# A decoder layer's attention, cross-attention and routed feed-forward on one core: packed score and value matmuls, folded norms, routing weights on the other side of the down projection

## What is computed

```python
x = x + _L0_attn_ref(_layernorm(x, axis=-1), L0_attn_Wqkv, L0_attn_bqkv, L0_attn_Wo, L0_attn_bo)
x = x + _L0_xattn_ref(_layernorm(x, axis=-1), ctx_1024, ctx_1024, L0_xattn_wq, L0_xattn_wk, L0_xattn_wv, L0_xattn_wo)
x = x + _L0_ffn_ref(_layernorm(x, axis=-1), L0_ffn_gate_w, L0_ffn_w_up, L0_ffn_w_down, L0_ffn_expert_bias)
...
scores = jnp.einsum('bhsd,bhtd->bhst', q, k) * (1.0 / math.sqrt(hd))
attn = jax.nn.softmax(scores, axis=-1)
vals = jnp.einsum('bhst,bhtd->bhsd', attn, v)
...
corr = jnp.fft.irfft(jnp.fft.rfft(Q, axis=-1) * jnp.conj(jnp.fft.rfft(K, axis=-1)), n=Lv, axis=-1)
top_vals, top_idx = jax.lax.top_k(corr, k_top)
...
w_t = jnp.sum(jnp.where(sel == e, top_scores, 0.0), axis=-1)
xe = xf * w_t[:, None]
h = jnp.square(jax.nn.relu(xe @ wu.T))
return (acc + h @ wd.T, None)
```

## Time and profile before

| | before |
|---|---|
| device time, median of 3 runs | 168.37 us (168.25 to 173.48) |
| span of the profiled execution | 171.5 us |
| PE busy | 153.6 us (90%), 1504 instructions |
| PEld busy | 128.2 us (75%) |
| DVE busy | 117.5 us (68%), 376 instructions |
| ACT busy | 72.5 us (42%), 153 instructions |
| POOL busy | 37.8 us (22%), 68 instructions |
| first `up` matmul starts | 93.55 us |

### The profile page before, as it was taken

How to read it: one execution, slowest core, us unless ns; L and a number is a source line. 1 busy time by engine, 2 the same in 40 slices (tenths; PEclk the granted TensorE clock), 3 DMA queues, 4 the chain that set the end, 5 groups by cost and what they waited for, 6 DMA issues and landing times.

```text
span 171.5 us, 3956 instructions
## 1 busy us (share of the span) xinstructions
PE 153.6 (90%) x1504; PEld 128.2 (75%) x1504; DVE 117.5 (68%) x376; ACT 72.5 (42%) x153; POOL 37.8 (22%) x68
## 2 busy tenths in 40 slices
PE   0439999999989987889997999999999999999992
PEld 0209777987978975478985799777998788978981
DVE  1197549676199699999989857684789856736340
ACT  2001422545544133544274960545506447347250
POOL 7126111020952201601420240005024120200000
PEclk9999999955799999999999999999999999999999
DMA  5996000000000000000000000000000010011001
GB/s 120 315 381 248 4 0 0 4 0 2 4 0 4 0 4 2 0 6 0 4 0 0 4 2 4 0 2 0 4 0 0 0 31 6 2 31 34 0 0 31
DMA packets 4391, 5.34 MB, mean 31 GB/s; under 512 B 380, under 2 KB 3708, under 8 KB 4116
## 3 DMA queue, kind: packets, MB, share of 16 engines
q1 hardware_dynamic: 3796, 3.95, 6.8%
q10 hardware_dynamic: 576, 1.14, 2.3%
HBM read 4.56 MB, written 0.52 MB: 30 GB/s over the span
## 4 chain that ended last, share of the span: by engine, by line
PE 70%; DVE 19%; issue 4%; POOL 3%; ACT 2%; DMA 2%; DVEq 0%; POOLq 0%
PE ps L877 13%; PE ps L866 12%; PE ps L740 10%; PE ps L768 8%; PE ps L748 3%; PE ps L709 3%; PE ps L851 3%; DVE xn L480 2%; PE ps L756 2%; DVE negm L535 2%; DMA x_sb<-x 2%; PE ps L806 2%; PE ps L703 1%; DVE rel L659 1%; PE ps L729 1%
## 5 line engine op out<-in xcount | busy, mean ns | idle before, releaser
L877 PE MATMUL ps<-hid,wdn_sb 128*128 128x256 f32 x128 | 32.0, 385 | 0.0
L659 DVE SCALAR_TENSOR_TENSOR rel<-ps,wb_sb 128x512 f32<-128x512 f32 x32 | 21.9, 689 | 10.3 <-PE ps L866 4.5
L740 PEld LDWEIGHTS ps<-feat 8*64 8x64 f32 x512 | 20.4, 165 | 7.1 <-DVE feat L521 4.2
L740 PE MATMUL ps<-feat 8*64 8x64 f32 x512 | 22.7, 255 | 3.0 <-DVE feat L521 3.0
L877 PEld LDWEIGHTS ps<-hid,wdn_sb 128*128 128x128 f32 x128 | 22.6, 190 | 3.6 <-issue 0.6
L452 ACT ACTIVATE hid<-rel 128x512 f32<-128x512 f32 x32 | 19.8, 630 | 10.1 <-PE ps L877 6.6
L866 PE MATMUL ps<-xhi,whi 128*128 128x256 f32 x64 | 20.9, 327 | 0.2 <-DVE praw L537 0.2
L866 PE MATMUL ps<-xlo,whi 128*128 128x256 f32 x64 | 17.9, 279 | 0.0
L866 PE MATMUL ps<-xhi,wlo 128*128 128x256 f32 x64 | 17.8, 279 | 0.0
L389 ACT ACTIVATE praw<-praw 128x512 f32<-128x512 f32 x16 | 10.1, 634 | 17.4 <-DVE praw L537 17.3
L535 DVE TENSOR_REDUCE negm<-ps 128x8 f32<-128x512 f32 x16 | 11.0, 686 | 9.5 <-PE ps L740 9.5
(11 more groups left out here) (112 smaller groups left out, 252.1 us busy)
## 6 DMA issues: line engine op xcount, KB each, us to landing
wup_sb<-w_up SPq DMA_DIRECT2D x1, 1024.0 KB, 11.3
wdn_sb<-w_down SPq DMA_DIRECT2D x1, 1024.0 KB, 10.1
c_sb<-ctxt SPq DMA_DIRECT2D x1, 512.0 KB, 8.7
out<-x_sb SPq DMA_DIRECT2D x4, 128.0 KB, 1.8
con<-consts ACTq DMA_DIRECT2D x1, 464.0 KB, 6.2
x_sb<-x SPq DMA_DIRECT2D x1, 384.0 KB, 9.5
wmid_sb<-w_mid ACTq DMA_DIRECT2D x1, 324.0 KB, 7.2
row_sb<-rows ACTq DMA_DIRECT2D x1, 260.0 KB, 4.9
```

The source lines that it names most:

```text
L659: nc.vector.scalar_tensor_tensor(rel[:, a % 2, :].rearrange("p (c t) -> p c t", c=2), psum(name, a).rearrange("p (c t) -> p c t", c=2), 0. ...
L740: last = mm(s_ps[cols, S * h:S * (h + 1)], feat[q:q + HD, 0, a % 2, g, h, :], feat[q:q + HD, 1, a % 2, g, h, :], start=True, stop=True)
L877: last = mm(acc_ps[:, 0:2 * P], wdn_sb[:, e, half, :], hid[:, a % 3, 2 * P * half:2 * P * (half + 1)], start=(e == 0 and half == 0), stop= ...
```

## The change

The program is written anew with one order table for each engine, and every step in them has its PSUM banks written behind it (`PE_ORDER` and its four companions). The order is no longer the same on all engines. What is computed where:

- Scores: the four strips of a chunk are one step. Its 64 matmuls go round the strips, innermost r, and the results of each strip go to a bank of its own (four banks).
- Values: the 32 `pv` matmuls go round the four groups of 32 output partitions; before, eight of one group stood in a row. The values of both column halves of a head ride in the free columns of the key's 32x32 blocks (`nat`), so that `fv` and half of `vtr` are gone, and ACT writes them into a `vkey` that POOL has zeroed once (L378).
- Softmax: for 12 of the 16 strips ACT copies the scores out of PSUM (`sev`, L363) and POOL subtracts the maximum (`psub`, L302); for the other four DVE does it as before (`ssub`). The exponential moves behind the transposes: ACT takes it straight from PSUM (L368), in place of an exponential and a copy.
- Norms: the first norm's centring is folded into the weights (`wc`: PE multiplies the weights by I - 1/128 once) and its scale into DVE's bias instruction (L488); the second's centring likewise into `wq`, its scale on ACT (`xs`, L399); the third is one ACT instruction with scale and shift for each tile (`xs3`, L422). DVE no longer normalises.
- Second block: the correlation runs as two halves of 64 rows into two banks (L759); the mixing matrix is built transposed by POOL (L309) from a DVE transpose (L585), so that `g` is gone.
- Third block: ACT does relu (L442) and square (L448); `up` weights are split by ACT and POOL alone. The down product takes the hidden units as its stationary side, four matmuls of 128 columns for each unit (L810), so that its rows are rows of x. DVE multiplies them by the squared routing weight and adds them to x (`mac`, L622, two for each unit). `wt`, `wb`, the accumulator's copy and `fin` are gone.

```diff
-                    if part == 0:
-                        pe.wait_ge(qkt_ready, 4 * (a + 1))
-                    s_ps, q = bank(name, a, part), 32 * part
+                    pe.wait_ge(done["ft"], NTH[("ft", a, 1)])
+                    bank(name, a)
                     for h in range(GROUPS):
                         for g in range(2):
-                            cols = slice(S * g, S * (g + 1))
-                            last = mm(s_ps[cols, S * h:S * (h + 1)], feat[q:q + HD, 0, a % 2, g, h, :],
-                                      feat[q:q + HD, 1, a % 2, g, h, :], start=True, stop=True)
-                    last.then_inc(score_full, 1)
+                            for r in range(QUAD):
+                                rows_r = slice(32 * r, 32 * r + HD)
+                                last = mm(psum(name, a, 0, r)[S * g:S * (g + 1), S * h:S * (h + 1)], feat[rows_r, a % 2, g, 0, h, :],
+                                          feat[rows_r, a % 2, g, 1, h, :], start=True, stop=True)
+                    last.then_inc(full[name], 1)
...
-                    for r in range(QUAD):
-                        pe.wait_ge(flip_free, QUAD * a + r + 1)
-                        for t in range(2):
-                            for i in range(PAIRS):
+                    for t in range(2):
+                        for i in range(PAIRS):
+                            for r in range(QUAD):
                                 last = mm(o_ps[32 * r:32 * r + 32, S * (PAIRS * t + i):S * (PAIRS * t + i + 1)],
-                                          vkey[:, a % 2, t, i, 32 * r:32 * r + 32], prob[:, a % 2, r, i, S * t:S * (t + 1)],
-                                          start=True, stop=True)
-                    last.then_inc(work_full, 1)
+                                          vkey[:, a % 2, t, i, r, :], prob[:, a % 2, r, i, S * t:S * (t + 1)], start=True, stop=True)
+                    last.then_inc(full[name], 1)
...
+                if name == "psub":
+                    pool.wait_ge(done["smax"], NTH[("smax", a, part)])
+                    pool.wait_ge(done["sev"], NTH[("sev", a, part)])
+                    both = praw[:, part].rearrange("p (h s) -> p h s", s=S)
+                    nc.gpsimd.tensor_tensor(both, both, negm[:, a, part, :].unsqueeze(2).broadcast_to([P, GROUPS, S]),
+                                            ALU.add).then_inc(done["psub"], 1)
...
+                if name == "wc":
+                    at = slice(A_QKV, A_Q) if a == 0 else slice(A_Q, A_GATE)
...
+                    mm(bank(name, a)[:, 0:at.stop - at.start], con[:, C_CEN:C_CEN + P], wa_sb[:, at], start=True,
+                       stop=True).then_inc(full[name], 1)
...
+                if name == "rel":
+                    u = EXPERTS * a + part
+                    act.wait_ge(full["up"], u + 1)
+                    if u >= 3:
+                        act.wait_ge(done["sq"], u - 2)
+                    nc.scalar.activation(rel[:, u % 3, :], psum("up", a, part), ACT.Relu).then_inc(done["rel"], 1)
...
-                    for half in range(2):
-                        last = mm(acc_ps[:, 0:2 * P], wdn_sb[:, e, half, :], hid[:, a % 3, 2 * P * half:2 * P * (half + 1)],
-                                  start=(e == 0 and half == 0), stop=(e == EXPERTS - 1 and half == 1))
-                    last.then_inc(down_done, 1)
...
+                    y_ps = bank(name, a, e)
+                    for t in range(2):
+                        for half in range(2):
+                            last = mm(y_ps[:, D * t:D * (t + 1)], hid[:, u % 3, 2 * P * half + P * t:2 * P * half + P * (t + 1)],
+                                      wdn_sb[:, e, half, :], start=(half == 0), stop=(half == 1))
+                    last.then_inc(full[name], 1)
...
+                        nc.vector.scalar_tensor_tensor(
+                            x12[:, 2 * a + t, :], psum("down", a, e)[:, D * t:D * (t + 1)], w2[:, a, t, e:e + 1],
+                            x12[:, 2 * a + t, :], ALU.mult, ALU.add).then_inc(done["mac"], 1)
```

```diff
+xt.0.0@0 wc.0.0@1 qkv.0.0@2 qkv.0.1@3 wc.1.0@4 xt.1.0@5 cdft.0.0@6 xt.2.0@7 qkv.1.0@0 cproj.0.0@1 qkv.1.1@2 score.0.0@4,5,3,6
...
+w8.0.0 st2.1.0 smax.3.0 smax.3.1 smax.3.2 pvt.2.0 smax.3.3 val.2.0 x2.0.0 ssub.3.0 st3.0.0 prod.1.0 x1.2.0 st2.2.0 top.1.0
```

More of the change, by code:

```diff
@@ L100 @@
[L100 to L125, removed]
@@ new lines, with steps @@
+rel.3.7 sq.3.6 sq.3.7
+"""
+POOL_ORDER = """
+zero.0.0 rs1.0.0 rs1.1.0 xb.0.0 rs1.2.0 wlo.0.0 psub.0.1 psub.0.2 psub.0.3 wlo.0.1 rs1.3.0 wlo.0.2 wlo.0.3 psub.1.1 psub.1.2
+psub.1.3 rs2.0.0 psub.2.1 psub.2.2 psub.2.3 mix.0.0 rs2.1.0 psub.3.1 psub.3.2 psub.3.3 rs3.0.0 rs2.2.0 xlo.0.0 mix.1.0 gs.0.0
+rs3.1.0 xlo.1.0 gs.1.0 mix.2.0 rs2.3.0 rs3.2.0 xlo.2.0 gs.2.0 mix.3.0 rs3.3.0 xlo.3.0 gs.3.0
+"""
+SP_ORDER = """
+sto.0.0 sto.1.0 sto.2.0 sto.3.0
+"""
+def steps(text):
+    found = []
+    for word in text.split():
+        step, _, banks = word.partition("@")
+        name, a, part = step.split(".")
+        found.append((name, int(a), int(part), tuple(int(b) for b in banks.split(",") if b)))
+    return found
@@ L142, in decoder_layer, with emptied_by @@
+def emptied_by(name, a, part, place):
+    if name == "score":
+        return ("sev" if (a, place) in BY_POOL else "ssub", a, place)
+    return (EMPTIES[name], a, part)
+def decoder_layer(nc, x, ctxt, w_cen, w_mid, w_up, w_down, rows, consts, out):
     with ExitStack() as ctx:
@@ L260, in decoder_layer @@
[L260 to L273 removed]
+        ld_x = [sem(f"ld_x{a}") for a in range(CHUNKS)]
@@ L459, in _ @@
+                if name == "sq":
+                    u = EXPERTS * a + part
+                    act.wait_ge(done["rel"], u + 1)
+                    if u >= 3:
+                        act.wait_ge(full["down"], u - 2)
+                    nc.scalar.activation(hid[:, u % 3, :], rel[:, u % 3, :], ACT.Square).then_inc(done["sq"], 1)
         @block.vector
         def _(dve):
-            chain = [0]
+            links = [0]
             def link(ins):
-                chain[0] += 1
+                links[0] += 1
@@ L808, in _ @@
-                    last.then_inc(work_full, 1)
-                if name == "g":
+                        for g in range(2):
+                            half = slice(64 * g, 64 * g + 64)
+                            last = mm(psum(name, a, 0, g)[:, 0:2 * L], prod[half, a % 2, i, :],
+                                      con[half, C_INV + 2 * L * i:C_INV + 2 * L * (i + 1)], start=(i == 0), stop=(i == 2))
+                    last.then_inc(full[name], 1)
+                if name == "ov":
+                    pe.wait_ge(done["cpe"], NTH[("cpe", a, 0)])
```

1011 lines of the change are left out of this document (476 added, 535 removed).

## The result

| | before | after |
|---|---|---|
| device time, median of 4 runs on one chip | 169.96 us (168.25 to 173.48) | 134.33 us (133.92 to 135.57) |
| ratio, 95% interval | | 0.799 (0.790 to 0.809) |
| span of the profiled execution (its own time) | 171.5 us (173.48) | 131.8 us (133.92) |
| first `up` starts | 93.55 us | 66.62 us |
| PE / DVE / ACT / POOL busy | 153.6 / 117.5 / 72.5 / 37.8 us | 114.3 / 89.7 / 77.2 / 46.9 us |

In kernel.py of the changed kernel the blank lines at the head are gone, so its lines are counted anew: scores are L692, values L718, `corr` L759, `up` L799, `down` L810 (PE), the accumulation with routing weights L622 (DVE), relu L442 and square L448 (ACT), the subtractions L302 (POOL).

What follows compares the result with a forecast made beforehand. The prediction took TensorE to bound the kernel, in work and clock speed: first stage 67, second stage 62 and end 2.6 make 131.6, forecast 131 us. The range for 8 in 10 was 121 to 149.

Steps and rivals of the forecast that it cites:

- 67 + 62 + 2.6: Whole kernel: first stage until the first up, second stage until the last down, then the end; 131.6 us together.
- I sum against 171.5 and give the forecast as the median: Whole kernel: terms summed against the profiled span, said to be 3.1 us above the runs' median of 168.37.
- foretold as 107 us: TensorE's work in the whole kernel at full clock: falls from 138 to 107 us, by 31.
- issue bound of 0.028 us: Scores and values: TensorE takes no instruction faster than 0.028 us; 8 us more, result 140; chance 0.20.
- The rule of the Trainium skill that was weighed: Scores: start-to-start never below about 25 ns, so 3.2 us a chunk instead of 2.0, sum about 137.
- 48 us of work at full clock, 12.7 lost at half clock, 6 idle: First stage: TensorE starts at 6 us, runs at half clock until 31.5, and ends its work at 67.
- From 6 us on as now: First stage: TensorE's 48 us of work would begin at 6 us, as in the kernel before.
- what would show it wrong: TensorE's clock: durations of equal instructions showing half clock after 35 us would be one sign against the forecast.
- later than DVE's 62, so PE's 67 counts: First stage: VectorE's chain allows the first up at 62, TensorE's work ends at 67, so TensorE sets it.
- DVE and POOL bind the first stage: First stage: 9 us of contention or late subtractions; first up at 69 to 72, result 134 to 137; chance 0.12.
- 59 us of work and 3 of waits: Second stage: 32 units of 1.6 us are 51, about 8 of leftover cross-attention, 3 added for waits.
- ScalarE comes up only below 1.22 us a unit: Second stage: ScalarE's relu and squares stay hidden unless a unit costs TensorE under 1.22 us; 1.6 was expected.

Runs made afterwards that it cites:

- scores_by_strip: Against the kernel after the change, the score matmuls go strip by strip, only a strip's two column halves taking turns: 143.38 us.
- sub_on_dve: Against the kernel after the change, all 16 maximum subtractions on VectorE, none on GpSimd, ScalarE's score copies gone, one residual and its statistics later: 145.16 us.
- values_by_group: Against the kernel after the change, the value matmuls go column group by column group again: 139.02 us.
- half_down: Against the kernel after the change, the down product takes only the first 128 of an expert's 256 hidden units: 128.68 us, unaltered 132.92.
- early_w: Against the kernel after the change, the first weights' transfer goes on ScalarE's queue ahead of the biases, extra products filling TensorE's waits: 133.18 us, unaltered 132.92.
- warm: Against the kernel after the change, 14 extra identity products of 128 columns in TensorE's wait for the first weights: 135.79 us.
- warm24: Against the kernel after the change, 24 extra identity products of 72 columns in TensorE's wait for the first weights: 141.2 us, unaltered 133.88.

## Why the prediction was right, and where not

**The sum.** 67 + 62 + 2.6 was foretold, 66.62 + 62.32 + 2.86 = 131.80 us is the span. The forecast of 131 is 3 us below the median all the same. The step that failed is "I sum against 171.5 and give the forecast as the median": 171.5 is a span, the time of that execution was 173.48, which is 5.1 us above the median of 168.37 and not 3.1. After the change the two are 131.8 and 133.92. The 2 us around the span belong to the time, and with them the sum is 133.6.

**TensorE's work.** All of it at full clock was foretold as 107 us and comes to 43.6 + 62.2 = 105.8 (the two stages are worked out below). Scores were taken at 2.0 us a chunk and measured 1.59, values at 1.4 and measured 1.10: tiles overlap more than the spacing of the earlier trace rows showed. `corr` was taken to fall to 3.0 in all and is 4 x 0.94 = 3.8. The two halves do run side by side: in the trace they start in pairs every 0.11 us, where one instruction of 256 columns started every 0.22 before. What doesn't halve is the last instruction's own time from start to end, 0.27 us, and the prediction halved that too. `down` is 0.90 us a unit, foretold 0.89: eight units in a row take 7.39 us with the last instruction's own end in it, and the starts of its instructions lie 0.112 us apart. The issue bound of 0.028 us fell: 11 ns lie between starts with eight tiles. The rule of the Trainium skill that was weighed, page "TensorE: Matmul & The Clock Gate", section "Wait — 56ns, not 53.3ns?", with starts never closer than about 25 ns, doesn't hold here for instructions on different tiles; with two tiles the 25 ns of `scores_by_strip` meet it as a mean only, for there they start in pairs 6 ns apart.

Of the parts of the change the runs undo three, one at a time: the packing of the scores (8 to 10 us), that of the values (3 to 6) and the move of the subtractions (about 11). The dropped transposes and the dropped spreading of routing weights, some 13 us of the earlier trace rows, and the folded norms were not undone; that they are part of the gain is argued, not shown by a run. In the second stage the traces speak for it: TensorE is busy there nearly throughout before and after (73.95 of 74.45 us, 62.17 of 62.32), so the time loses what its work loses.

**The first stage came out at 67 by luck: three errors cancel.** Foretold: 48 us of work at full clock, 12.7 lost at half clock, 6 idle. Measured: the four stretches at half clock hold 17.1 us of busy PE, so 8.6 lost; 52.16 - 8.6 = 43.6 of work; 66.62 - 52.16 = 14.5 idle. Against the forecast that is 4.4 and 4.1 us less and 8.5 more. "From 6 us on as now" failed: the projection waits for centred weights, and their transfer lands at 7.2. The pause of 2.3 us was not foreseen. The clock rose at 15.4 us, not 31.5, and fell three times later, twice behind 35 us, which the prediction named as what would show it wrong.

**What sets the first stage.** The step "later than DVE's 62, so PE's 67 counts" failed in its first half. VectorE's work up to the third statistics was right: 43.62 us busy at 61.07 against 43 + 2.5.

```profile
0.00:61.07 61.07, 46.90 (x911) 37.70 (x912) 43.62 (x118) 29.41 (x71) 30.99 (x41) 0.92 0.24 74
```

Its idle time was not: 17.4 us instead of 12, of it 2.83 behind the paused scores. From the statistics to `up` it takes 5.55 us, not 4.5. VectorE's chain therefore ends at 66.6, no room left, and it and TensorE take turns in holding each other up (VectorE waits 3.6 us for scores and 3.3 for projections after 9 us; TensorE's longest wait for VectorE is 0.7 us here and 3.1 in `sub_on_dve`). In all kernels but `values_by_group` the first `up` starts 3.56 or 3.57 us after ScalarE begins to scale the third norm. That was the premise of the rival "DVE and POOL bind the first stage", without its price: subtractions took 1.06 us instead of 1.47, and the contention was near the 2.5 us taken. VectorE and GpSimd, in order of time:

```profile
48.01 0.42 DVE L533 TENSOR_TENSOR vals<-onat,rden 128x256 f32<-128x256 f32 x1
...
58.50 1.02 DVE L533 TENSOR_TENSOR vals<-onat,rden 128x256 f32<-128x256 f32 x1
59.44 0.41 DVE L589 TENSOR_TENSOR x<-ps,x 128x256 f32<-128x256 f32 x1
```

```profile
57.20 3.22 POOL L302 TENSOR_TENSOR praw<-praw,negm 128x512 f32<-128x512 f32 x3
```

Beside GpSimd's subtractions the division of two SBUF operands takes 1.02 us for 0.42; the addition with a PSUM operand keeps its 0.41. The Trainium skill, page "SBUF — State Buffer", section "Who interferes with whom", says that VectorE's instructions with two SBUF inputs and GpSimd's that read SBUF shut each other out of a shared pair of ports; these rows agree.

**The second stage.** Foretold: 59 us of work and 3 of waits. Measured: 62.2 of work and none. By the spacing in their runs a unit's `up` takes 0.71 and its `down` 0.90 us, 51 us in 32 units as foretold; what is left is 11 us where 8 were taken. The 3 us put down as waits thus were work, and the sum is right because both errors are of one size. `mac` is 0.345 us (taken 0.279, bound 0.689) and relu 0.592, both hidden. The statement that ScalarE comes up only below 1.22 us a unit was too hopeful: `half_down` shows 5 us of cover, after which the chunks' own chain binds.

## What to carry to other kernels

Small matmuls on four tiles in turn were nearly as good as on eight here, and both shift the bound elsewhere: work out the dependent chain over the other engines with its waits, not its busy time alone. A dense run of tiny instructions can outrun the instruction fetch; a pause with no releaser that stays at the same instruction count when code is put ahead points to that. And a cover of "TensorE is busy all the time" is only as deep as the next chain allows, which leaving out a known amount of its work measures.

## What the runs showed of the hardware

- TensorE's instructions arrive in blocks of 256 as the trace counts them. Blocks used up in 1.4 to 2.6 us were followed by pauses of 0.7 to 2.3 us, but of 0.3 us in `values_by_group`, where the next block's packet had started within 0.4 us. Slower blocks of 4.5 and 4.9 us, in `early_w` and `warm`, were followed by 2.2 us, since the packet started 4.2 and 4.7 us after the crossing. TensorE resumes 1.3 to 1.5 us after the packet's end.
- One program, profiled three times, has the first `up` at 64.0, 66.6 and 66.9 us, with granted clocks of 0.95, 0.92 and 0.87 up to there. What brings the half-clock stretches on isn't settled. `values_by_group` had almost no pause in the second scores and full clock up to about 52 us, but `scores_by_strip` had none either and low clock for much of the first stage (0.78).
- Instructions of 72 columns with weights of 128 x 128 came every 0.213 us in `warm24`, no closer than those of 128 columns at that clock.
